# Source rows, places and weight rests of a scatter's preparation made by GpSimd, first keys written directly

## What is computed

```python
edge_index = jnp.stack([src, dst])
h = jnp.maximum(_layernorm(x), 0.0)
W = zeros((1024, 1024)).at[src, dst].add(edge_weight)     # row, col = edge_index
x = x + h @ W.T + bias
h = jnp.maximum(_layernorm(x), 0.0)
# two layers, each with the mean over incoming edges:
#   agg = segment_sum(h[src], dst); h @ W_self + (agg / deg) @ W_neigh + b
x = x + sage(relu(sage(h)))
```

## Time and profile before

| | us |
|---|---|
| median of 3 runs | 772.57 (772.55 to 772.92) |
| span of the profiled execution | 771.7 |
| TensorE busy | 749.4 (97%) |
| VectorE, ScalarE, GpSimd busy | 570.8, 353.9, 479.4 |

### The profile page before, as it was taken

How to read it: one execution, slowest core, us unless ns; L and a number is a source line. 1 busy time by engine, 2 the same in 40 slices (tenths; PEclk the granted TensorE clock), 3 DMA queues, 4 the chain that set the end, 5 groups by cost and what they waited for, 6 DMA issues and landing times.

```text
span 771.7 us, 13501 instructions
## 1 busy us (share of the span) xinstructions
PE 749.4 (97%) x4433; PEld 620.0 (80%) x4434; DVE 570.8 (74%) x814; ACT 353.9 (46%) x596; POOL 479.4 (62%) x593
## 2 busy tenths in 40 slices
PE   3999999999999999999999999999999999999998
PEld 2878888888888888888788888888888888887886
DVE  7999587778464887977778685356497857579885
ACT  7867733334253352357436645442223333244731
POOL 5000267667659899955657283327799975645992
PEclk9999999999999999999999999999999999999999
DMA  3123367676486853566683536786744768785475
GB/s 116 43 79 103 116 192 244 216 240 190 144 260 205 290 175 121 191 205 239 208 285 122 183 99 187 221 279 204 264 139 137 233 218 279 238 277 181 151 238 200
DMA packets 82985, 148.78 MB, mean 193 GB/s; under 512 B 10809, under 2 KB 21108, under 8 KB 82912
## 3 DMA queue, kind: packets, MB, share of 16 engines
q1 hardware_dynamic: 62974, 105.18, 43.2%
q10 hardware_dynamic: 19938, 42.69, 15.7%
HBM read 106.42 MB, written 41.41 MB: 192 GB/s over the span
## 4 chain that ended last, share of the span: by engine, by line
PE 94%; DVE 2%; POOL 1%; issue 1%; ACT 1%; DMA 0%; DVEq 0%; ACTq 0%; POOLq 0%
PE bank L1730 50%; PE bank L1780 21%; PE bank L1664 13%; PE bank L1557 4%; PE bank L1547 1%; PE bank L1578 1%; PE bank L1796 1%; PE bank L1568 1%; PE bank L1657 1%; PE bank L1574 1%; POOL narrow L1053 1%; DMA dst_g<-in_dst 0%; DVE st L1912 0%; PE bank L1592 0%; ACT asum L1292 0%
## 5 line engine op out<-in xcount | busy, mean ns | idle before, releaser
L1730 PE MATMUL bank<-slot,split 128*128 128x512 f32 x1128 | 261.7, 390 | 0.6 <-issue 0.5
L1730 PEld LDWEIGHTS bank<-slot,split 128*128 128x128 f32 x1128 | 210.8, 188 | 44.6 <-issue 1.4
L1073 POOL TENSOR_TENSOR AT<-AT,az 128x50 int32 (+3 forms) x288 | 96.8, 336 | 111.1 <-DMA az<-asum_scratch 71.2
L1730 PE MATMUL bank<-slot,split_third 128*128 128x512 f32 x552 | 129.7, 390 | 0.3 <-DVE cst L2336 0.3
L1730 PEld LDWEIGHTS bank<-slot,split_third 128*128 128x128 f32 x552 | 103.1, 188 | 21.9 <-DVE cst L2336 0.5
L1780 PE MATMUL bank<-slot,Ax 128*128 128x512 f32 x500 | 119.0, 392 | 0.2
L2100 DVE TENSOR_TENSOR slot<-T,slot 128x512 fp32r<-128x512 f32 x64 | 84.8, 1334 | 36.1 <-ACT slot L1333 32.1
L1780 PEld LDWEIGHTS bank<-slot,Ax 128*128 128x128 f32 x500 | 92.8, 188 | 20.3 <-issue 1.4
L1664 PE MATMUL bank<-slot,split_m 128*128 128x512 f32 x320 | 91.1, 396 | 0.0
L1129 POOL TENSOR_TENSOR T<-T,wst 128x512 f32<-128x512 f32 x48 | 64.9, 1371 | 4.8 <-DMA wst<-in_L_gnn_W_self 4.8
L1664 PEld LDWEIGHTS bank<-slot,split_m 128*128 128x128 f32 x320 | 58.5, 188 | 11.1
(11 more groups left out here) (230 smaller groups left out, 1198.8 us busy)
## 6 DMA issues: line engine op xcount, KB each, us to landing
stage<-hT_scratch SPq DMA_DIRECT2D x90, 256.0 KB, 3.7
wst<-in_L_gnn_W_neigh SPq DMA_DIRECT2D x56, 256.0 KB, 4.2
wst<-in_L_gnn_W_self SPq DMA_DIRECT2D x56, 256.0 KB, 3.3
x1b_scratch<-x ACTq DMA_DIRECT2D x10, 512.0 KB, 5.8
hT_scratch<-hTs ACTq DMA_DIRECT2D x10, 512.0 KB, 3.1
wst<-prod0g_scratch SPq DMA_DIRECT2D x20, 256.0 KB, 3.4
hT_scratch<-h1s ACTq DMA_DIRECT2D x20, 256.0 KB, 3.2
wst<-prod1g_scratch SPq DMA_DIRECT2D x20, 256.0 KB, 3.2
```

The lines of the kernel that those rows point to most:

```text
L1073: pool.tensor_tensor(a, a, az32[:, n % NZ, pairs * pos:pairs * (pos + 1)], ALU.add) \
L1730: last = pe.matmul(dense_bank(v, which)[:, :], split_tile(v, a)[:, NT * k:NT * (k + 1)], slot[t % 2][:, b, HF * (HK * which + k):HF * (HK ...
```

## The change

GpSimd takes over, between its constants and its wait for the first R: `slo` in two steps, `whole` in two steps, and the rests of the weights in four, the first eight groups (`FIRST`) apart from the other 32. `slo` and `whole` are int32 now. ScalarE makes the parts of the weights in the same split, in an order that follows GpSimd's (`s_prep` counts its eight steps, `s_tile` tells it that `tile_of` is there). VectorE no longer makes `slo`, `rest` and `whole`; it writes `key2` of the first eight groups directly from `whole` and the spread firsts, and makes the full `key` behind the weighing of group 0. A further edit clamps a register in a loop that this input doesn't enter (`further_windows`).

```diff
+            pool.wait_ge(s_tile, 1)
+            pool.tensor_scalar(slo[:, :, :], tile_of[:, :, :], -float(NT), None, ALU.mult).then_inc(s_prep, 1)
+            pool.wait_ge(s_prep, 1)
+            pool.tensor_tensor(slo[:, :, :], slo[:, :, :], src_c[:, :, :], ALU.add).then_inc(s_prep, 1)
+            pool.wait_ge(s_edge[2], 16)
+            pool.tensor_scalar(whole[:, :, :], dst_c[:, :, :], float(TN), None, ALU.mult).then_inc(s_prep, 1)
+            def weight_rest(half, part):
+                groups = parts_of_w[half]
+                pool.wait_ge(s_wc, 3 * half + part + 1)
+                if part:
+                    pool.wait_ge(s_prep, PREPARED[f"rest{2 * half}"])
+                pool.tensor_tensor(rest[:, groups, :], (rest if part else w_c)[:, groups, :], w2[:, groups, :, part, 0],
+                                   ALU.subtract).then_inc(s_prep, 1)
+            weight_rest(0, 0)
+            pool.wait_ge(s_prep, PREPARED["places"])
+            pool.tensor_tensor(whole[:, :, :], whole[:, :, :], tile_of[:, :, :], ALU.add).then_inc(s_prep, 1)
+            weight_rest(0, 1)
+            weight_rest(1, 0)
+            weight_rest(1, 1)
             pool.wait_ge(s_R, 1)
...
-            dve.wait_ge(s_dve, tile_done)
-            dve.scalar_tensor_tensor(out=slo[:, :, :], in0=tile_of[:, :, :], scalar=-float(NT), in1=src_c[:, :, :],
-                                     op0=ALU.mult, op1=ALU.add).then_inc(s_key, 1)
...
-            dve.tensor_tensor(rest[:, :, :], w_c[:, :, :], w2[:, :, :, 0, 0], ALU.subtract).then_inc(s_wp, 1)
...
-            placed = tick(dve.scalar_tensor_tensor(out=whole[:, :, :], in0=dst_c[:, :, :], scalar=float(TN),
-                                                   in1=tile_of[:, :, :], op0=ALU.mult, op1=ALU.add))
...
-            dve.tensor_tensor(key[:, :, :], whole[:, :, :], firsts_of_edges(), ALU.subtract).then_inc(s_key, 1)
-            dve.wait_ge(s_wc, 2)
-            dve.wait_ge(s_wp, 1)
-            dve.tensor_tensor(rest[:, :, :], rest[:, :, :], w2[:, :, :, 1, 0], ALU.subtract).then_inc(s_wp, 1)
...
+                    dve.wait_ge(s_prep, PREPARED["whole"])
+                    dve.wait_ge(s_span, 1)
+                    each = [EP, FIRST, GC, 2]
+                    dve.tensor_tensor(key2[:, 0:FIRST, :, :], twice(whole[:, 0:FIRST, :], FIRST),
+                                      firsts_of_edges()[:, 0:FIRST, :].unsqueeze(3).to_broadcast(each),
+                                      ALU.subtract).then_inc(s_key, 1)
...
+                if j == 0:
+                    dve.tensor_tensor(key[:, :, :], whole[:, :, :], firsts_of_edges(), ALU.subtract).then_inc(s_key, 1)
```

More of the change, by code:

```diff
@@ L230, in build_program @@
         tile_of = sb("tile_of", [EP, NG, GC], I32, build)
-        whole = sb("whole", [EP, NG, GC], F32, build)
+        whole = sb("whole", [EP, NG, GC], I32, build)
         rest = sb("rest", [EP, NG, GC], F32, build)
-        slo = sb("slo", [EP, NG, GC], F32, build)
+        slo = sb("slo", [EP, NG, GC], I32, build)
         key = sb("key", [EP, NG, GC], F32, build)
@@ L720, in further_windows @@
                             k = nc.s_assert_within(k, 1, NK - 1, skip_runtime_bounds_check_because=clamped)
[L721 to L722 removed]
+                            eng.reg_alu(nth, less + k, 1, ALU.max)
+                            nth_now = nc.snap(nth, engines=bass.OrderedEngineSet([eng.engine]))
+                            body(b, k, nc.s_assert_within(nth_now, 1, NG * NK, skip_runtime_bounds_check_because=clamped))
                 if then is not None:
@@ L727, in twice @@
             return a.unsqueeze(3).to_broadcast([EP, groups, GC, 2])
+        PREPARED = {what: n + 1 for n, what in enumerate(("part of slo", "slo", "places", "rest0", "whole", "rest1", "rest2", "rest3"))}
+        parts_of_w = [slice(0, FIRST), slice(FIRST, NG)]
         def rows_of(i):
@@ L1256, in _, with weight_part @@
             act.wait_ge(s_edge[3], 16)
-            act.copy(w2[:, :, :, 0, :], twice(w_c[:, :, :], NG)).then_inc(s_wc, 1)
-            act.wait_ge(s_key, 1)
+            def weight_part(half, part):
+                groups = parts_of_w[half]
+                last, to = (w_c if part == 0 else rest)[:, groups, :], w2[:, groups, :, part, :]
+                act.copy(to, twice(last, groups.stop - groups.start)).then_inc(s_wc, 1)
+            weight_part(0, 0)
+            act.wait_ge(s_prep, PREPARED["slo"])
             act.copy(slo2[:, :, :, :], twice(slo[:, :, :], NG)).then_inc(s_twice, 1)
+            act.wait_ge(s_prep, PREPARED["rest0"])
+            weight_part(0, 1)
             act.wait_ge(s_low, 2)
@@ L1262, in _ @@
             act.activation(tab_ag[:, :], first[:, :], ACT.Copy, scale=float(TN // 2)).then_inc(s_tabg, 1)
-            act.wait_ge(s_wp, 1)
-            act.copy(w2[:, :, :, 1, :], twice(rest[:, :, :], NG)).then_inc(s_wc, 1)
+            act.wait_ge(s_prep, PREPARED["rest1"])
+            weight_part(0, 2)
+            weight_part(1, 0)
+            act.wait_ge(s_prep, PREPARED["rest2"])
+            weight_part(1, 1)
             act.wait_ge(s_key, 2)
[L1266 to L1269, removed]
             act.copy(key2[:, FIRST:NG, :, :], twice(key[:, FIRST:NG, :], NG - FIRST)).then_inc(s_twice, 1)
+            act.wait_ge(s_prep, PREPARED["rest3"])
+            weight_part(1, 2)
             act.copy(slo2_late[:, :, :, :], twice(slo[:, LATE:NG, :], LG)).then_inc(s_slate, 1)
```

20 lines of the change are left out of this document (9 added, 11 removed).

## The result

The changed kernel takes 774.95 us (median of 15 runs, 773.78 to 775.58) against 773.07 (15 runs, 772.03 to 774.12) of the kernel before in the same rounds. The ratio is 1.0021 with a 95% interval of 1.0014 to 1.0028, so it is slower by about 1.6 us (1.1 to 2.2). The forecast of 773.2 had the sign; the time lies above its range, and the loss is more than twice the +0.65 us of its sum.

The account below looks back on a forecast made before the run. TensorE's start, set by `tab_g`, two transfers and register loads, was taken as the bound. -0.40 saved plus 0.10, 0.55 and 0.40 of waits gave +0.65 on 772.57, so 773.2 us, range 772.0 to 774.5.

Parts of the forecast that it names:

- the +0.65 us of its sum: Predicted delay of `tab_g`, passed on to the kernel's end: -0.40 + 0.10 + 0.55 + 0.40.
- What bounds the kernel: TensorE's start: VectorE's preparation to `tab_g`, two transfers, register loads; VectorE's groups beside it with 0.6 us slack at group 0.
- What the change removes: VectorE's `slo` ahead of `tab_g`: -0.40 us on the path, some 2.0 us off VectorE's queue.
- The price of GpSimd's multiply: GpSimd's one-input multiply on 320 columns: 0.45 us, bounded by 0.18 and 0.89.
- The lock: GpSimd's new steps hold VectorE's two-input SBUF steps: +0.10 at `base_r`, +0.55 at third `first`, +0.40 at `firsts_d`.
- "4.2 us behind `tab_g`": TensorE's first group follows `tab_g` by an unchanged 4.2 us of transfers and register loads, at about 13.4.
- Condition (2): VectorE's group 6 late beyond `tab_g`'s shift plus some 0.1 us adds the excess; predicted 0.45 late, hidden.
- VectorE gets through: Rival: GpSimd's addition misses the third `first` step, `firsts_d` meets the short rest; -0.4 to +0.2 us, chance 0.26.
- GpSimd starves: Rival: GpSimd's last rest, `before` and `narrow` come late, group 6 late by 1.1 to 1.6 us; chance 0.11.
- Dearer on integers: Rival: GpSimd's int32 sums take 1.53 us, `tab_g` 2.5 to 3.0 late; 0.09 including other losses above +1.55.
- The range: Predicted time 772.0 to 774.5 us, holding the forecast and first two rivals, leaving dearer integers out.

Follow-up runs that it names:

- late_tab_g: The kernel before with two more VectorE instructions like `slo`, whose results nobody needs, ahead of the chain that ends in `tab_g`; ratio 1.0017 to the kernel before.
- after: The changed kernel as measured and profiled, against the kernel before: 774.95 us, ratio 1.0021.
- tables_first: The changed kernel with ScalarE's two table copies moved ahead of its wait for GpSimd's first `rest`; ratio 1.0018 to the kernel before.
- prices: The kernel before with twelve GpSimd instructions on spare data at its queue's head; multiply by a constant on 320 columns 1.01 us, integers and floats.
- both_late: The kernel before with VectorE's chain 0.85 us longer and ScalarE's clearing 3.2 us later, GpSimd unchanged; ratio 1.0010 to the kernel before.
- slo_behind: The changed kernel with `slo` back on VectorE but behind `tab_g`, and ScalarE's table copies first; ratio 1.0017 to the kernel before.

## Why the prediction was wrong

- **What bounds the kernel: right.** TensorE's start follows `tab_g`, the two transfers and the loads, and VectorE's groups run beside it. late_tab_g put +1.04 us ahead of `tab_g` and got +1.03 at the first group; the wait that the chain of waits names, VectorE's at `narrow`, is gone in after, and nothing is faster.
- **What the change removes: -0.40 forecast, -0.29 found.** The slot of `slo` had also covered 0.11 us of the wait for the reduction that `limit` reads.
- **The price of GpSimd's multiply: the term that was mis-sized.** 0.45 us with an upper bound of 0.89, from a selection on 128 columns and one on a single column; it is 1.01 alone and 1.03 to 1.04 here. These rows were of another operation, and a bound taken from them bounded nothing. Its sums were right within 0.04. Both multiplies together are 1.17 us longer than forecast, and so the sums meet other steps of VectorE than the forecast listed.
- **The lock: the mechanism right, its places wrong.** It had +0.10, +0.55 at the third `first` step and +0.40 at `firsts_d`. Found: +0.08 at the second `first`, off the path; nothing at the third; +0.59 at `limit`; +0.17 at the last `first`, where "at most 0.1, taken as nothing" stood; nothing at `firsts_d`. That is 0.76 on the path for 1.05. `tab_g` came at +0.47 for +0.65, in truth earlier than forecast.
- **"4.2 us behind `tab_g`": the step that failed.** It was 4.66 (13.62 - 8.96). The forecast let `tab_w` follow `tab_o`, and traced ScalarE's queue only at its far end, where the clearing is. But the copies that write the table stand in that queue too, and the change put a wait for GpSimd ahead of them. With the short multiply the first `rest` would have been done at about 8.1 (an estimate: the rows of after with 0.45 for each multiply and 0.36 for the `rest`), long before SyncE was free at 9.80; with the real one, and held by VectorE's first step of group 0, it was done at 9.75. One mis-sized term and one queue not walked through gave the other +0.44 to +0.46; tables_first took 0.41 of it back on the clock, 0.46 counted from `low`.
- **Condition (2): right in its verdict, wrong in its rows.** The weighing of group 0 ended 0.05 us earlier relative to `low`, not 0.4, since `key` waited 1.04 us for `whole`. GpSimd was not starved: `narrow` found its gap at 16.20. VectorE's weighing of group 6 ended at 21.89 against TensorE's 22.69, so nothing of it shows.
- **The rivals.** "VectorE gets through" did not happen in the sum, though two of its locks fell away. "GpSimd starves" did not happen. "Dearer on integers" was wrong as a mechanism (prices), yet the time that it stood for, above the range, is nearly what came.
- **The range.** The start, which is what the failed steps above explain, came +0.91 us late in three traces, 0.26 more than the +0.65 of the sum; the interval of the first comparison starts at 1.1. Of what is left, some 0.7 us at the middle by the ratio, the loads at 28 us explain a part in some executions, and the rest is **open**: both_late, with nearly the same start, took +0.8, but its interval overlaps that of after. The forecast also stood on the median of three runs, 772.57; fifteen runs of the same kernel gave 773.07. So of the 1.75 us by which it missed, 0.26 is the start, 0.50 the base, and 0.97 (medians: 1.88 less 0.91) the part that stays open. A range that ended 1.3 us above its middle left no room for these.

The forecast gave 0.90 to a difference within 0.2% and 0.09 to slower by more. 1.6 us lies at that bound.

## What to carry to other kernels

When work moves to another engine, walk through every queue that waits for it, to the end, and ask of each what else stands behind that wait: here two tiny copies behind a weight part cost as much as the contention. Price a step only from rows of the same operation; where there is none, an unlike row is a guess and not a bound. And taking work off an engine gains nothing while another chain, here a table, two small transfers and the loads of registers, sets the start.

## What the runs showed of the hardware

- **GpSimd's operation with a constant is dearer than its sum of two operands.** The multiply takes 1.01 us for 320 columns against 0.72 to 0.86 for the sum, and 0.37 for 64 columns against 0.29, on integers and floats alike; the addition of a constant takes 0.38 for 64. The Trainium skill, GPSIMD Engine Reference, section 4.1 Engine selection, sets GpSimd beside VectorE and calls one-input operations roughly line-rate and two-input ones about twice as slow. Here it is the other way round: the multiply took 3.3 times VectorE's one-input `tile_of`, a shift on the same shape (0.31), the sum 1.3 to 1.5 times VectorE's `rest` (0.57), and the measurement decides.
- **The hold between VectorE and GpSimd isn't always for the whole instruction.** `limit` waited to the end of the sum (0.74 for 0.15), and GpSimd's multiply stood behind two VectorE steps in slo_behind (1.80 for 1.03). But the `first` of 6.37 and the `firsts_d` of 8.40, both with two inputs, ran at full speed beside a multiply of GpSimd that was 0.69 and 0.65 us old and had 0.35 and 0.38 to go. A multiply held only what came in its first tenths of a microsecond (the `first` of 5.88, +0.08, and of 7.79, +0.17). The Trainium skill, SBUF — State Buffer, section Who interferes with whom, gives the lock to whoever issues first, for the whole instruction: so it is with the sums, and not with these multiplies.
- **A step of VectorE with one tensor and a scalar for each partition waits too.** `general_d`, three columns, took 0.83 us beside the last `rest` of GpSimd, 0.21 before; the `first` of 7.79 is such a step as well.
- **A register load of TensorE's queue takes 0.59 us in the median and up to 1.00 beside a small store**, and 42 of them stand on the path of the edge stage: their sum was 24.45 to 26.34 us between executions and moved TensorE by as much. One load of 0.85 us, at 17.2 to 19.1 us, is in every one of these traces without a store beside it.
- **The landing of the first input varies.** `low` started at 3.64 to 4.09 us in the twelve traces of the table, and at 3.79, 3.95 and 4.08 in the three of after alone, so that two spans of one kernel can differ by a third of a microsecond before anything is computed.
